# Attention phase: the slots of every engine's stages placed anew

## The reference, cut to what matters

```python
x = L0_attn_q                                                    # [16, 512, 128]
x = x + 0.5 * _L0_ffn_ref(_layernorm(x), theta, phi, ...)        # sqrt((x cos W)^2 + (x sin W')^2)
x = x + _L0_attn_ref(_layernorm(x), Wq, Wk, Wv, Wo)
x = x + 0.5 * _L0_ffn_ref(_layernorm(x), theta, phi, ...)
x = x + 0.5 * _L1_ffn_ref(_layernorm(x), gate_w, gate_b, ...)    # only its gate is in this phase
...                                                              # mixer and last part: other phases
def _L0_attn_ref(q, Wq, Wk, Wv, Wo):
    xq, xk, xv = rope(q @ Wq), rope(q @ Wk), q @ Wv              # 16 heads of 64, 8 distinct for k and v
    scores = softmax(xq @ xk * scale)
    return (scores @ xv) @ Wo
```

## Time and profile before

| | |
|---|---|
| time, median of 3 runs | 2530.32 us (2524.23, 2530.32, 2531.66) |
| span of the profiled execution | 2524.8 us (no other time of it is given) |
| PE busy | 2163.5 us, 86% |
| DVE busy | 1827.8 us, 72% |
| POOL busy | 1455.5 us, 58% |
| ACT busy | 1410.7 us, 56% |
| mean granted clock of the PE | 0.957 |

### The profile page before, as it was taken

One profiled execution on the slowest core, in us unless ns is written; L12 is line 12 of the kernel. 1 busy time (PEld: TensorE's weight loads), 2 busy tenths in 40 slices (PEclk: granted clock), 3 DMA queues, 4 the chain that ended last, 5 costly groups with the idle time before them and its releaser, 6 DMA issues. The chain is left out here.

```text
span 2524.8 us, 39953 instructions
## 1 busy us (share of the span) xinstructions
PE 2163.5 (86%) x14226; PEld 994.3 (39%) x14226; DVE 1827.8 (72%) x4240; ACT 1410.7 (56%) x2651; POOL 1455.5 (58%) x1264
## 2 busy tenths in 40 slices
PE   3689989989889889989989998569898899898878
PEld 1223333333323333323323322236566566665534
DVE  5777777777777777777777773358888888887668
ACT  2166566566566566566566566254555655556234
POOL 3366666665665665665665645146555656565358
PEclk9799999999999999999999999689999999999789
DMA  3221211112112112112112120100000000000033
GB/s 116 55 49 38 50 36 46 47 35 51 42 34 51 43 34 56 38 34 58 35 34 59 31 69 9 30 13 22 26 22 26 26 22 26 22 18 14 14 100 109
DMA packets 86598, 103.70 MB, mean 41 GB/s; under 512 B 10240, under 2 KB 68736, under 8 KB 86272
## 3 DMA queue, kind: packets, MB, share of 16 engines
q1 hardware_dynamic: 86400, 101.16, 15.3%
HBM read 29.55 MB, written 20.97 MB: 20 GB/s over the span
## 5 line engine op out<-in xcount | busy, mean ns | idle before, releaser
L347 DVE TENSOR_REDUCE mS<-ps 128x1 f32<-128x512 f32 x1024 | 676.9, 681 | 301.8 <-PE ps L724 297.3
L506 ACT ACTIVATE pr<-ps 128x512 f32<-128x512 f32 x1024 | 585.9, 597 | 383.7 <-PE ps L708 365.6
L579 POOL TENSOR_TENSOR prs<-pr 128x512 f32<-128x512 f32 x384 | 487.3, 1288 | 243.3 <-ACT pr L506 243.3
L708 PE MATMUL ps<-qst,kst 97*128 97x512 f16 x1024 | 397.2, 391 | 53.3 <-ACT pr L506 52.2
L724 PE MATMUL ps<-kst,qst 96*128 96x512 f16 x1024 | 400.4, 392 | 36.6 <-DVE mS L347 25.7
L746 PE MATMUL ps<-pr,vt 128*32 128x512 f32 x2048 | 279.6, 619 | 0.0
L708 PEld LDWEIGHTS ps<-qst,kst 97*128 97x128 f16 x1024 | 99.1, 98 | 419.3 <-ACT pr L506 307.3
L583 POOL TENSOR_TENSOR terms<-terms 128x512 f32<-128x512 f32 x128 | 162.4, 1268 | 69.3 <-DVE terms L340 69.3
L340 DVE TENSOR_TENSOR terms<-ps,shared 128x512 f32<-128x512 f32 x256 | 173.1, 678 | 34.9 <-POOL lo L588 29.7
L588 POOL TENSOR_TENSOR lo<-terms,hi 128x512 f16<-128x512 f32 x128 | 148.0, 1156 | 76.9 <-ACT hi L486 76.9
L724 PEld LDWEIGHTS ps<-kst,qst 96*128 96x128 f16 x1024 | 101.1, 99 | 150.4 <-DVE mS L347 80.1
(11 more groups left out here) (267 smaller groups left out, 4399.2 us busy)
## 6 DMA issues: line engine op xcount, KB each, us to landing
qst<-hi SPq DMA_DIRECT2D x128, 128.0 KB, 2.4
kst<-hi SPq DMA_DIRECT2D x128, 128.0 KB, 2.4
qst<-lo SPq DMA_DIRECT2D x64, 128.0 KB, 2.4
kst<-lo SPq DMA_DIRECT2D x64, 128.0 KB, 2.4
x<-in_q SPq DMA_DIRECT2D x16, 256.0 KB, 2.8
shared<-in_rope SPq DMA_DIRECT2D x1, 4096.0 KB, 14.4
x<-yold SPq DMA_DIRECT2D x16, 256.0 KB, 2.5
n<-kept SPq DMA_DIRECT2D x16, 256.0 KB, 2.1
```

The source lines that it names most:

```text
L347: v.tensor_reduce(mS[:, b % 2, t, s:s + 1], ps[:, 2 + n % 2, :], AX, ALU.max).then_inc(S["s_read"], 1)
L506: a.activation(pr[:, s % 2, g, :], ps[:, g % 2, :], ACT.Exp, scale=ATT_SCALE).then_inc(S["exp"], 1)
L579: g.tensor_tensor(prs[:, c, :], pr[:, 0, c, :], pr[:, 1, c, :], ALU.add).then_inc(S["prs"], 1)
L708: mm(ps[:, g % 2, :], kst[:, h, P * kt:P * kt + P], qst[:, h, :], start=True, stop=True).then_inc(S["st"], 1)
```

## The change

Each stage of each engine gets its own table of slots, in which a number of 64 or more means a slot of the following iteration (`due` yields these first). Nothing that is computed changes, nor does the waiting of any stage on another: only the order in which each engine's list holds its instructions. On the lists the following moves (slots before and after):

- PE: score tiles 3, 4, 15 to 17, 20 and 46 to 52 go ahead of one shifted tile (16 and 49 of more); values 5 and 6 from slot 25 and 29 to 27 and 31; sums 5 from 51 to 52; direct sums 1 from 59 to 57; values 15 and direct sums 3 from the end of the iteration to slot 0 of the next, after the first shifted tile and score tile.
- DVE: maximum 26 ahead of both residuals; maximum 7 ahead of the second half of the first statistics, and their aggregation ahead of maximum 8; maxima 46 to 52 each ahead of the gate count or product that they followed; the last division's first part at the end of slot 63, its second a slot earlier.
- ACT: second part of the first normalisation ahead of exponential 12; first evacuation ahead of exponential 17; exponential 32 ahead of the second normalisation; the copy for the next phase from slot 50 to 45; high part 4 ahead of exponential 52; numerators 3 ahead of high part 7.
- POOL: pair sum 13 ahead of the second deviations; rotated sum 5 ahead of low part 4; the next phase's low part ahead of low part 5.

The diff, cut to its core (the engines' other loops ask `due` in the same way):

```diff
 ATTENTION_AT = {
-
-    "values": (0, 1, 7, 8), "output": 4, "x2": 4, "stats1": 5, "aggr1": 8, "xn1": 11, "turn1": 16, "evac1": 17,
-    "ffn": 18, "squares": 19, "ffn_b": 22, "squares_b": 22, "sqrt": 25, "resid": 25, "stats2": 27, "aggr2": 29,
-    "xn2": 31, "turn2": 36, "evac2": 35, "gate": 37, "gate_in": 37, "next_hi": 50, "next_lo": 55, "gate_top": 41, "gate_count": 45,
-    "project": (37, 38, 39, 40, 41, 42, 45, 46, 47, 49, 50, 51, 53, 56, 59, 60), "high_lag": 3, "low_lag": 2,
-    "denominators_lag": 3, "maxima": 5,
+        "scores": (0, 1, 2, 2, 3, 5, 6, 7, 8, 9, 10, 11, 12, 13, 14, 14, 14, 15, 18, 19, 19, 21, 22, 23, 24, 25, 26,
+        27, 28, 29, 30, 31, 32, 33, 34, 35, 36, 37, 38, 39, 40, 41, 42, 43, 44, 45, 45, 46, 47, 47, 49, 50, 51, 53,
+        54, 55, 56, 57, 58, 59, 60, 61, 62, 63),
+        "reduce": (0, 1, 2, 3, 4, 5, 6, 7, 8, 9, 10, 11, 12, 13, 14, 15, 16, 17, 18, 18, 19, 21, 22, 23, 24, 25, 26,
+        27, 28, 29, 30, 31, 32, 33, 34, 35, 35, 36, 38, 39, 40, 41, 42, 43, 44, 45, 46, 47, 48, 49, 50, 51, 52, 53,
+        54, 55, 56, 57, 58, 59, 60, 61, 62, 63),
+    "maxima": 5,
+    "values": (5, 9, 13, 17, 21, 27, 31, 33, 37, 41, 45, 49, 53, 57, 61, 64),
+    "pair_sums": (4, 5, 6, 7, 12, 13, 14, 15, 20, 21, 22, 23, 27, 27, 30, 31, 36, 37, 38, 39, 44, 45, 46, 47),
+    "sums": (11, 19, 27, 35, 43, 52),
+    "sums_directly": (55, 57, 63, 64),
+    "numerators": (19, 35, 51, 63),
+    "divide": (21, 22, 23, 37, 38, 39, 53, 54, 55, 63, 64, 66),
+    "project_values": (0, 1, 7, 8),
+    "evac_values": (0, 1, 7, 8),
+    "output": 4,
+    "x2": 4,
+    "stats1": (5, 7),
+    "aggr1": 7,
+    "rstd1": 9,
+    "xn1": (11, 11, 13, 14),
+    "turn1": 16,
+    "evac1": 16,
+    "ffn": (18, 18, 22, 22),
+    "squares": (19, 19, 22, 22),
+    "add_squares": (19, 19, 22, 22),
+    "sqrt": 25,
+    "resid": (26, 26),
+    "stats2": (27, 28),
+    "aggr2": 29,
+    "rstd2": 29,
+    "xn2": (32, 32, 33, 34),
+    "turn2": 36,
+    "evac2": 35,
+    "low_input": 36,
+    "gate": 37,
+    "gate_in": 37,
+    "gate_top": 41,
+    "gate_count": 46,
+    "next_hi": 45,
+    "next_lo": 53,
+    "project": (37, 38, 39, 40, 41, 42, 45, 46, 47, 49, 50, 51, 53, 56, 59, 60),
+    "rotate": (38, 39, 40, 41, 42, 43, 47, 48, 49, 51, 52, 52, 54, 57, 60, 61),
+    "rotated": (39, 41, 43, 47, 50, 50, 55, 61),
+    "high": (41, 43, 45, 49, 51, 54, 59, 63),
+    "low": (40, 41, 43, 48, 51, 53, 58, 62),
 }
...
-        product_at = {q + 1: m for m, q in enumerate(AT["project"])}
-        rotated_at, high_at, low_at = ({q + lag: m // 2 for m, q in enumerate(AT["project"]) if m % 2}
-                                       for lag in (1, AT["high_lag"], AT["low_lag"]))
-        assert max(high_at) < SLOTS
+
+        def due(name, q):
+
+            table = AT[name] if isinstance(AT[name], tuple) else (AT[name],)
+            return [(k, late) for late in (1, 0) for k, at in enumerate(table) if at == q + SLOTS * late]
...
-        def maximum_at(i, q):
-
-            m = SLOTS * (i - 1) + q - LAG
-            return m if 0 <= m < BATCH * SLOTS else None
-
-        def guard_at(i, q):
-            m = SLOTS * (i - 1) + q - LAG
-            half = SLOTS // 2
-            return m // half - 1 if 0 < m <= BATCH * SLOTS and m % half == 0 else None
+        def maxima_at(name, i, q):
+
+            for k, late in due(name, q):
+                m = SLOTS * (i - late - 1) + k - LAG
+                half = SLOTS // 2
+                yield (m if 0 <= m < BATCH * SLOTS else None,
+                       m // half - 1 if 0 < m <= BATCH * SLOTS and m % half == 0 else None)
...
-                        s, t = q // NT, q % NT
-                        if maximum_at(i, q) is not None:
-                            maximum(maximum_at(i, q))
-                        if guard_at(i, q) is not None:
-                            guard_row(guard_at(i, q))
-                        if is_att(i) and s % NG == 1 and s > NG and t:
-                            divide(i - 2, s // NG - 1, t - 1)
-                        if is_old(i) and q < 3:
-                            divide(i - 3, NG - 1, q)
+                        for tile, guard in maxima_at("reduce", i, q):
+                            if tile is not None:
+                                maximum(tile)
+                            if guard is not None:
+                                guard_row(guard)
+                        for k, late in due("divide", q):
+                            if is_att(i - late):
+                                divide(i - late - 2, k // 3, k % 3)
...
-                        if is_new(i) and q in product_at:
-                            if i == 0 and product_at[q] == 0:
-                                dve.wait_ge(S["place_in"], 16)
-                            product(i, product_at[q])
-                        if i == 0 and q == AT["aggr1"] + 1:
+                        for k, late in due("rotate", q):
+                            if is_new(i - late):
+                                if i == 0 and k == 0:
+                                    dve.wait_ge(S["place_in"], 16)
+                                product(i - late, k)
...
                         s, g = q // NG, q % NG
                         if is_att(i):
                             exponentials(i - 2, s, g)
-                            if q in AT["values"]:
-                                t = AT["values"].index(q)
-                                act.wait_ge(S["v_ps"], NT * (i - 2) + t + 1)
+                        for t, late in due("evac_values", q):
+                            if is_att(i - late):
+                                act.wait_ge(S["v_ps"], NT * (i - late - 2) + t + 1)
                                 a.copy(vt[:, t, :], ps[:, 5, :]).then_inc(S["v"], 1)
-                            if s and s % NG == 0 and g == 3:
-                                numerators(i - 2, s // NG - 1)
+                        for j, late in due("numerators", q):
+                            if is_att(i - late):
+                                numerators(i - late - 2, j)
                         for part in range(4):
...
-                        if maximum_at(i, q) is not None:
-                            scores(maximum_at(i, q))
-                        if guard_at(i, q) is not None:
-                            guard_row(guard_at(i, q))
-                        if is_att(i) and s and t == 1:
-                            values(i - 2, s - 1)
-                        n, lag = q // (2 * NT), q % (2 * NT)
-                        if is_att(i) and 0 < n < HEADS // 2 - 1 and lag == AT["denominators_lag"]:
-                            denominators(i - 2, n - 1)
-                        if is_att(i) and s > HEADS - NT and t == 3:
-                            denominators_directly(i - 2, s - 1)
-                        if is_att(i) and q in AT["values"]:
-                            project_values(i - 2, AT["values"].index(q))
+                        for tile, guard in maxima_at("scores", i, q):
+                            if tile is not None:
+                                scores(tile)
+                            if guard is not None:
+                                guard_row(guard)
+                        for k, late in due("values", q):
+                            if is_att(i - late):
+                                values(i - late - 2, k)
+                        for n, late in due("sums", q):
+                            if is_att(i - late):
+                                denominators(i - late - 2, n)
+                        for k, late in due("sums_directly", q):
+                            if is_att(i - late):
+                                denominators_directly(i - late - 2, HEADS - NT + k)
+                        for k, late in due("project_values", q):
+                            if is_att(i - late):
+                                project_values(i - late - 2, k)
                         if is_old(i) and q == AT["output"]:
```

More of the change, by code:

```diff
@@ L533, in _ @@
                             transposed(i, 1)
-                        if q == AT["squares"]:
-                            for k in range(2):
-                                squares(i, k)
-                        if q == AT["squares_b"]:
-                            for k in range(2, len(tiles(i)) // 2):
+                        for k, _ in due("squares", q):
+                            if k < len(tiles(i)) // 2:
                                 squares(i, k)
@@ L550, in _ @@
                             a.copy(kept[:, 0], xnTo[:, :]).then_inc(S["kept_hi"], 1)
-                        if is_new(i) and q in high_at:
-                            high(i, high_at[q])
-                    if is_att(i):
-                        numerators(i - 2, NG - 1)
+                        for p, late in due("high", q):
+                            if is_new(i - late):
+                                high(i - late, p)
             @block.gpsimd
@@ L593, in _ @@
```

(49 more changed lines are left out.)

14 lines of the change are left out of this document (8 added, 6 removed).

## The result

The changed kernel takes 2493.5 us (median of 4 runs, 2492.5 to 2493.9) against 2530.4 (4 runs, 2524.2 to 2531.7): a ratio of 0.9857, 95% interval 0.9844 to 0.987, or 1.4% less. The profiled span is 2490.3 us, 34.5 less. The forecast was 2501, with a range of 2484 to 2520.

What follows compares the result with a forecast made beforehand. The PE bounds the kernel. Terms of -2.15, -0.3 and -0.1 us a batch, plus 0.5 for the clock, give -2.05 over 13 batches and -2 for partial ones: -29 us off the median 2530.3, 2501 us, range 2484 to 2520.

Steps and rivals of the forecast that it cites:

- The bound: Whole batch: the PE is the bound; matmuls stay unchanged, so at most its idle 9.3 us a batch can be won.
- The batch boundary: Values 15 and last denominators after the next batch's first two score tiles: 0 us, between -0.2 and +0.5.
- its 48.65: Slot 36: the transposes start 48.65 us into the batch, from 51.23 and 49.99 in the two batches before.
- Slots 6 to 18: Earlier statistics, early score tiles and evacuation: -0.1 us a batch, between -0.4 and +0.5.
- Slots 25 to 36: Three orders (DVE, POOL, ACT) bring the first projection earlier: -2.96 and -1.34 us, -2.15 in the mean.
- Slots 45 to 52: Early tiles and projection 11 ahead of the pair-sum wait: -0.3 us a batch, between +0.5 and -0.9.
- The clock: Half clock (1.2 GHz) on the PE's path in every third batch, at 1.6 us: +0.5 us a batch.
- rival 1: Half clock stays on the path in every batch, as every batch has such a stretch now: 2516 us; chance 0.2.
- The sum: -2.55 us a batch without half clock, +0.5 for it: -2.05 x 13, -2 for partial batches, -29 us, 2501 us.
- Rival 2: Half clock never lies on the path: -2.55 us x 13 - 3 = -36, 2494 us; chance 0.17.
- rival 3: Half clock on the path twice a batch, at slots 15 to 17 or 46 to 51, and 35: 2541 us; chance 0.09.
- Rival 4: Orders fail: another wait holds tile 36 or the gate as long as before; -0.4 us a batch, 2525 us; chance 0.09.

Runs made afterwards that it cites:

- the two experiments: Kernel before with only maximum 26, exponential 32 and pair sum 13 moved ahead: 2502.1 us; changed kernel with these three orders put back: 2510.4 us.
- the single ones: Changed kernel with one order put back each: exponential 32, 2502.0 us; maximum 26, 2504.3 us; pair sum 13 (with 12), 2502.6 us.
- the first experiment: Kernel before with three orders alone: maximum 26 ahead of residuals, exponential 32 of second normalisations, pair sum 13 of second deviations; 2502.1 us, ratio 0.9903.

## Why the prediction was right, and where it was off

- *The bound.* Right: the PE's matmuls stayed (x480 or 481 in each batch), its idle time paid for all of it. In batches without a clock stretch it was 93.13 - 83.03 = 10.10 before and is 90.98 - 83.20 = 7.78 after, while busy time hardly moved. The 8.6 us of idle time that the earlier trace rows give for the second batch are fewer because its matmuls at the lower clock take longer and count as busy (84.58 for 83.03).
- *The batch boundary.* Right at 0 (+0.03). The output projection starts 768.70 - 762.17 - 1.86 = 4.67 us in, 4.63 before; no stack is waited for in slot 5. The prediction forgot, though, that the swap moves the mark from which it counted: its 48.65 has to be compared with 48.12.
- *Slots 6 to 18.* Mis-sized: -0.1, measured -0.67. The step was "comes 0.5 later and ends some 0.2 ahead of tile 14, its reader: nothing". It followed exponential 12, which does come 0.4 later, and not the list behind it: the 0.4 us by which the normalisations start earlier is kept by what ACT does from exponential 13 to slot 18, and by itself takes 0.44 off the PE's waits of 0.64 and 0.16. The early tiles with the evacuation, priced as new waiting that the old wait covers, bring as much by themselves: two tiles of 0.22 go ahead of the wait.
- *Slots 25 to 36.* Right in mechanism, a little large: -1.34 for a batch without the clock on its path, measured -1.16 (1.15 and 1.17 by the two experiments). All three orders take part, as the single ones show. The wait for pair sums went; what is late next, tile 35 for exponential 33, stands 1.14 us where the prediction had 1.5.
- *Slots 45 to 52.* Right: -0.3, measured -0.26, with the named new waits (0.42 at tile 46 in this batch and, with the long copy, 0.65 in the mean, for 0.55; 0.30 at projection 11 for 0.45; 0.08 at projection 8 for 0.2). That the early tiles lose and that the stretch wins more without them was not seen.
- *The clock.* The net term came out (-0.31, measured -0.32) by luck. The clock itself gave more, some -0.5 (0.85 to 0.32), and the DVE's long copy, which the prediction did not have, took 0.2 back. The form was off too: not one stretch on the path in three batches but stretches in 4 of 13. One batch has 10.2 us of them and the long copy (94.82); in the others a stretch of 3.4 us costs 0.4 to 0.5 (92.62 is 0.50 for the stretch and 1.15 for the copy). Nor did "every batch" have a stretch before, as rival 1 says: the batches at 309.07 and 496.96 have none.
- *The sum.* -2.05 a batch forecast, -2.48 measured: 0.57 too little in slots 14 to 18, 0.18 too much in the chain, the rest in slots 45 to 63. 13 x 0.43 = 5.6 of the 7.5 us between 2501 and 2493.5. Rival 2 gave 2494, but for another reason (no clock stretch at all), and does not hold: the profile after has them. Rival 1 (in every batch) and rival 3 (twice a batch) fall with stretches in 4 batches of 13, though one stretch did come where rival 3 saw it, in slots 45 and 46. Rival 4 falls with the first experiment.

Not settled: the first shifted tile comes at 128.9 us, 2.2 later than before. With the old start it came at 126.7 and 127.5 (the first experiment), with the new one between 127.8 and 132.0. The change may cost a microsecond or more there, but the spread is larger than that, and it was not tested.

## What to carry to other kernels

Where engines run lists in order, cut the batch of both kernels at the same matmuls and compare stretch by stretch; mind that a moved instruction may cross the mark. An order that lets an engine run something ready inside a wait is worth at most that something's length to everyone behind it, up to the next wait of theirs, and must be followed that far (here 0.48 us for an exponential that holds ACT for 0.48, 0.38 for a maximum of 0.68, 0.58 for a pair sum of 1.27). An early tile helps where the PE will wait anyway and nothing else waits for its engine; elsewhere (slots 45 to 52) it only moves the wait to a place where it delays others, and where another engine's delay, such as the long copy, reaches the PE.

## What the runs showed that I had not expected

The lower clock does not follow the PE's idle time. The three orders alone leave 91.97 - 83.02 = 8.95 us of a batch idle and show no such stretch in 13 batches; the changed kernel leaves 7.78 and shows them in 4; the kernels with one order put back show them in 8, 8 and 11, mostly 6.8 us from slot 30 or 31. All of them wait in the same stretch, slots 25 to 36. These counts are of one execution each, and executions differ: the mean granted clock of the first experiment was 0.967 in the profiled one and 0.959 to 0.963 in its other three. What decides is open. And a stretch may cost nothing: with pair sum 13 put back, a batch with 3.4 us at the lower level and one without take the same time, as the PE is busier (84.50 to 82.95) by what it waits less:

```profile
213.63:305.19 91.56, 84.50 (x481) 29.94 (x477) 68.42 (x154) 58.68 (x109) 58.06 (x50) 0.98 0.18 44
...
1228.92:1320.47 91.55, 82.95 (x480) 29.86 (x477) 68.41 (x154) 58.78 (x109) 58.00 (x50) 1.00 0.19 44
```
